# Dividing a finished attention block: from a ScalarE copy, a VectorE reciprocal and a GpSimd product to VectorE alone, straight from PSUM

## The reference

```python
scores = jnp.einsum('bhnd,bhmd->bhnm', q, k) / sqrt(Dh)
attn = jax.nn.softmax(scores, axis=-1)
sa = jnp.einsum('bhnm,bhmd->bhnd', attn, v)
sa = sa.transpose(0, 2, 1, 3).reshape(bs, N, H * Dh)
out = jnp.einsum('bnd,ed->bne', sa, w_agg) + b_agg
```

## Time and profile before

| what | value |
|---|---|
| median of 3 runs | 1554.31 us (1553.98 to 1554.68) |
| the profiled execution's own time | 1566.26 us |
| its span, first to last instruction | 1564.0 us |
| mean granted TensorE clock | 0.934 of full speed |
| busy: PE, DVE, ACT, POOL | 1364.3, 1062.3, 869.9, 564.2 us |
| instructions: PE, DVE, ACT, POOL | 10311, 2037, 1251, 1142 |

### The profile page before, as it was taken

How to read it: one execution, slowest core, us unless ns; L and a number is a source line. 1 busy time by engine, 2 the same in 40 slices (tenths; PEclk the granted TensorE clock), 3 DMA queues, 4 the chain that set the end, 5 groups by cost and what they waited for, 6 DMA issues and landing times.

```text
span 1564.0 us, 27948 instructions
## 1 busy us (share of the span) xinstructions
PE 1364.3 (87%) x10311; PEld 912.5 (58%) x10311; DVE 1062.3 (68%) x2037; ACT 869.9 (56%) x1251; POOL 564.2 (36%) x1142
## 2 busy tenths in 40 slices
PE   4777989999999999999999999999988988886563
PEld 3534555666566666665666566656655555564452
DVE  3325684859585958596858685868598899746711
ACT  1244656666767666766666666666646555521110
POOL 1311530335133503350345034503431051656663
PEclk8888999999999999999999999999999988978775
DMA  2034002600360036013500360036000640344442
GB/s 74 2 92 110 1 28 64 181 14 15 80 178 14 28 71 173 14 29 80 164 14 28 80 164 14 28 78 166 14 1 16 160 135 1 109 149 137 127 138 69
DMA packets 66014, 119.07 MB, mean 76 GB/s; under 512 B 10321, under 2 KB 46162, under 8 KB 65874
## 3 DMA queue, kind: packets, MB, share of 16 engines
q1 hardware_dynamic: 56640, 92.04, 22.1%
q0 software_dynamic: 8192, 25.17, 5.3%
q10 hardware_dynamic: 1042, 0.01, 0.0%
HBM read 29.11 MB, written 33.55 MB: 40 GB/s over the span
## 4 chain that ended last, share of the span: by engine, by line
PE 55%; DVE 22%; issue 7%; ACT 5%; POOL 4%; SPq 2%; another core or an unknown queue 2%; DMA 1%; DVEq 0%; ACTq 0%; POOLq 0%
PE shared L873 29%; PE scores L829 10%; PE acc L851 9%; DVE prob_sum L1489 9%; PE shared L868 3%; ACT probs L1123 3%; DVE acc_sb L1474 2%; PE acc L861 2%; PE acc L848 1%; DVE bn L1249 1%; DVE best_i L1406 1%; DVE work L1408 1%; DVE best L1404 1%; SPq L465 1%
## 5 line engine op out<-in xcount | busy, mean ns | idle before, releaser
L1123 ACT ACTIVATE probs<-scores 128x1024 f32<-128x1024 f32 x512 | 516.0, 1022 | 218.6 <-DVE prob_sum L1489 127.7
L1489 DVE TENSOR_TENSOR prob_sum<-prob_sum,probs 128x512 f32<-128x512 f32 x640 | 420.6, 717 | 0.3 <-issue 0.3
L829 PE MATMUL scores<-query_stack,key_stack 96*128 96x256 f32 x2048 | 344.6, 308 | 49.5 <-ACT probs L1123 45.5
L829 PEld LDWEIGHTS scores<-query_stack,key_stack 96*128 96x128 f32 x2048 | 278.7, 194 | 125.6 <-ACT probs L1123 77.4
L851 PE MATMUL acc<-probs,v_all 128*32 128x256 f32 x4096 | 296.2, 397 | 0.0
L1156 POOL TENSOR_TENSOR attn_T<-acc_sb 128x256 f32<-128x256 f32 x64 | 55.5, 866 | 522.7 <-DVE acc_sb L1474 515.5
L873 PE MATMUL shared<-w_sb,chan 128*128 128x512 f32 (+1 forms) x512 | 185.4, 503 | 5.3 <-DVE chan L1310 5.0
L851 PEld LDWEIGHTS acc<-probs,v_all 128*32 128x32 f32 x4096 | 116.0, 112 | 98.2 <-issue 31.2
L1489 DVE TENSOR_TENSOR prob_sum<-probs 128x512 f32<-128x512 f32 x128 | 97.0, 799 | 59.3 <-PE acc L861 55.3
L873 PEld LDWEIGHTS shared<-w_sb,chan 128*128 128x128 f32 x512 | 92.8, 193 | 66.3 <-issue 56.5
L1474 DVE RECIPROCAL acc_sb<-acc_sb 128x256 f32<-128x256 f32 x64 | 111.5, 1742 | 26.6 <-ACT acc_sb L1113 26.5
(11 more groups left out here) (168 smaller groups left out, 1955.9 us busy)
## 6 DMA issues: line engine op xcount, KB each, us to landing
query_stack<-hi SPq DMA_DIRECT2D x128, 128.0 KB, 2.4
key_stack<-hi SPq DMA_DIRECT2D x128, 128.0 KB, 2.5
x_sb<-in_x_dram SPq DMA_DIRECT2D x8, 1024.0 KB, 5.8
key_stack<-lo SPq DMA_DIRECT2D x64, 128.0 KB, 2.5
query_stack<-lo SPq DMA_DIRECT2D x64, 128.0 KB, 2.5
out_dram<-resid SPq DMA_DIRECT2D x16, 512.0 KB, 4.9
tokens_scratch<-resid SPq DMA_DIRECT2D x16, 512.0 KB, 6.3
tokens_scratch<-rows SPq DMA_DIRECT2D x16, 512.0 KB, 6.5
```

Of the source, the lines that this page charges most:

```text
L829: last = pe.matmul(score_ps[u % 2][:, QB * r:QB * (r + 1)], key_stack[stack, HG * g + r, P * kt:P * (kt + 1)], query_stack[stack, HG * g + ...
L1123: act.activation(probs[:, u % PROBS, :], score_ps[u % 2][:, :], ACT.Exp, scale=DH ** -0.5) \
L1489: dve.tensor_tensor(total[:, part], probs[:, (u - 1) % PROBS, part] if kt == 1 else total[:, part], probs[:, u % PROBS, part], ALU.add).th ...
```

## The change

VectorE's `divide` takes the place of three pieces: `copy_acc` on ACT, `invert` on DVE and `divide` on POOL. It waits for `blocks_done`, takes the reciprocal of the bank's right half from PSUM into a new small buffer `sum_r`, waits for its own `recip_ready`, and multiplies the bank's left half, again from PSUM, with `sum_r` into `attn_T`. PE waits for `attn_ready` where it waited for `acc_copied`. For the first four blocks of a batch it must not overwrite `attn_T` while `agg` of the batch before reads it: POOL waited, at the first of them, for the last two tiles of `agg`; DVE waits at each of the four for the two tiles that this block overwrites.

```diff
@@ tensor: weigh
                 if kt == 0 and blk >= 2:
-                    pe.wait_ge(s["acc_copied"], blk - 1)
+                    pe.wait_ge(s["attn_ready"], blk - 1)
@@ scalar
-            def copy_acc(blk):
-                act.wait_ge(s["blocks_done"], blk + 1)
-                await_count(act, "attn_ready", blk)
-                act.activation(acc_sb[:, :], acc_ps[blk % 2][:, :], ACT.Copy) \
-                   .then_inc(s["acc_copied"], 1)
...
-                if k and k % BLOCK_PAIRS == 0:
-                    copy_acc(k // BLOCK_PAIRS - 1)
@@ gpsimd
-            def divide(blk):
-                a, g, qb = blk // (G * NQB), blk % (G * NQB) // NQB, blk % NQB
-                pool.wait_ge(s["recip_ready"], blk + 1)
-                if a and blk % (G * NQB) == 0:
-                    storing = next(seg for seg in segments if seg.has("store") and seg.stores == a - 1)
-                    for t in range(T - 2, T):
-                        await_read(pool, storing, "agg", t)
-                pool.tensor_tensor(attn_T[:, g, QB * qb:QB * (qb + 1)], acc_sb[:, 0:QB],
-                                   acc_sb[:, QB:2 * QB], ALU.mult).then_inc(s["attn_ready"], 1)
...
-                if k and k > BLOCK_PAIRS and k % BLOCK_PAIRS == 1:
-                    divide(k // BLOCK_PAIRS - 1)
@@ vector
-            def invert(blk):
-
-                dve.wait_ge(s["acc_copied"], blk + 1)
-                dve.reciprocal(acc_sb[:, QB:2 * QB], acc_sb[:, QB:2 * QB]).then_inc(s["recip_ready"], 1)
+            def divide(blk):
+                a, g, qb = blk // (G * NQB), blk % (G * NQB) // NQB, blk % NQB
+                dve.wait_ge(s["blocks_done"], blk + 1)
+                if a and g == 0:
+                    storing = next(seg for seg in segments if seg.has("store") and seg.stores == a - 1)
+                    for t in range(QB // P * qb, QB // P * (qb + 1)):
+                        await_read(dve, storing, "agg", t)
+                acc = acc_ps[blk % 2]
+                dve.reciprocal(sum_r[:, :], acc[:, QB:2 * QB]).then_inc(s["recip_ready"], 1)
+                dve.wait_ge(s["recip_ready"], blk + 1)
+                dve.tensor_tensor(attn_T[:, g, QB * qb:QB * (qb + 1)], acc[:, 0:QB], sum_r[:, :], ALU.mult) \
+                   .then_inc(s["attn_ready"], 1)
...
                 if k and k % BLOCK_PAIRS == 0:
-                    invert(k // BLOCK_PAIRS - 1)
+                    divide(k // BLOCK_PAIRS - 1)
```

More of the change, by code:

```diff
@@ L360, in build_attention @@
     prob_sum = sb("prob_sum", [P, HG * QB])
-    acc_sb = sb("acc_sb", [P, BANK])
+    sum_r = sb("sum_r", [P, QB])
     head_ones = env["head_ones"]
@@ L417, in build_attention @@
              "stats_ready x_stats_ready z2_ready maxima_ready resid_ready dve_done one_row_in summed "
-             "blocks_done acc_copied norm_squared bound_ready shift_known attn_ready recip_ready").split()
+             "blocks_done norm_squared bound_ready shift_known attn_ready recip_ready").split()
     sems = {n: ctx.enter_context(nc.semaphore(n)) for n in names}
@@ L660, in build_segments @@
      qT, z2T, qk0, dots_sb, sumv_sb, x_sum, bn6, bn_x, mv, mv_x, small, ss, hr, hh, ln_v, ln_r, ln_h, ln_b,
-     prob_sum, acc_sb, head_ones, norm_sq, norm_max, pair_max, bound, shifted, logits_sb, score_ps, acc_ps,
+     prob_sum, sum_r, head_ones, norm_sq, norm_max, pair_max, bound, shifted, logits_sb, score_ps, acc_ps,
      shared_ps) = (env[k] for k in (
@@ L664, in build_segments @@
         "qT z2T qk0 dots_sb sumv_sb x_sum bn6 bn_x mv mv_x small ss hr hh ln_v ln_r ln_h ln_b "
-        "prob_sum acc_sb head_ones norm_sq norm_max pair_max bound shifted logits_sb score_ps acc_ps "
+        "prob_sum sum_r head_ones norm_sq norm_max pair_max bound shifted logits_sb score_ps acc_ps "
         "shared_ps").split())
@@ L1133, in _ @@
                     exponential(2 * k + 2)
-                elif units and n and plan[n - 1].pair == pairs - 1:
-                    copy_acc(units // T - 1)
                 for st in first:
@@ L1234, in _ @@
                 k = slot.pair
-                if units and k is None and n and plan[n - 1].pair == pairs - 1:
-                    divide(units // T - 1)
-                if k and k > BLOCK_PAIRS and k % BLOCK_PAIRS == 1:
-                    divide(k // BLOCK_PAIRS - 1)
                 for st in slot.steps:
@@ L1495, in _ @@
                 if units and k is None and n and plan[n - 1].pair == pairs - 1:
-                    invert(units // T - 1)
+                    divide(units // T - 1)
                 for st in first:
```

## The result

The changed kernel took 1561.6 us (median of 11 runs, 1558.0 to 1563.2), the kernel before 1554.3 us (median of 11, 1550.5 to 1559.3): a ratio of 1.0043, 95% interval 1.0031 to 1.0056. On another chip, where the kernel before stood at 1575.0 us, the ratio was 1.0052 (1.0035 to 1.0070). The change makes the kernel some 7 us slower.

A forecast was written before the change was run, and what follows sets the result against it. PE was taken as the bound in the long run, with the chain often leaving it for DVE; +10.4 (DVE's product) - 2.4 (copy wait) - 1.7 (POOL relief) = +6.3 us on 1554.3 gave 1560.6 us, range 1553 to 1567.

The forecast's parts named there:

- DVE's product: The division's multiply, moved to DVE: +0.45 us for each block, +10.4 us over 23 places on the chain.
- The 23 places: Blocks of 64 whose reciprocal stands on the chain, two in each repeating segment (slots 0 and 12); each pays 0.45 us.
- the rival of the absorbed delay: Chain places in repeating segments run into cover the chain doesn't show: sum +1.8 us, 1556.1 us, no change; chance 0.26.
- the ten places: Chain places in the repeating segments after the first segment; without them the sum was put at 6.3 - 4.5 = +1.8 us.
- The pause that it named: PE's idle time at the end of slot 12's chain, 0.78 us before, expected near 1.2 after.
- POOL's product: 64 x 866 ns leave POOL, 55.5 us; claimed that nothing on the chain gets earlier by that alone.
- The relief term of -1.7 us: DVE's sums no longer stretched 0.46 us beside POOL's product, at four chain places in the last three segments and the first.
- PSUM: Reading reciprocal and product operands from PSUM: taken as 0, bounds -0.7 to +2.6 us over the 23 places.
- The rival of dear PSUM reads: Reciprocal and product each cost 57 ns more from PSUM: +2.6 us, 1563.2 us, or 1567.3 without relief; chance 0.12.
- The wait for the copy: DVE no longer waits for ACT's copy; gains at three chain places (192.88, 1356.68, 1367.39 us), -2.4 us in sum.
- Its rival: DVE's 26.5 us of waiting for the copy reaches PE; with half of it 1549.7 us, faster; chance 0.12.
- PE's new wait for `attn_ready`: PE waits for the block two back, set three slots ahead; costs nothing unless DVE falls back by three slots.

The follow-up runs named there:

- The doubled product: Changed kernel, with each block's product made a second time by DVE into a tile that nothing reads; ratio 1.0153 to the kernel before, body 1013.5 us.

## Why the prediction was right, and where its steps failed

The time (1560.6 forecast, 1561.6 measured) and the sign came out. That the number is so near is luck: the stretch that the profile can compare has +8.0 us in the repeating segments, where the forecast has +5.4, and -1.7 in the rest up to the last `total`, where it has +0.9. The two misses cancel.

- **DVE's product, +0.45 us at a place on the chain.** Right as a price: 0.42 us from a row of 0.41, and at slot 0 it gave +0.51 us in each segment, with PE's wait at 1.02 us for a forecast of 0.95. The doubled product gave 0.29 to 0.34 us more in the periods where the clock stayed up.
- **The count of places on the chain.** The 23 places are those of one chain, and the prediction put the 41 others beside other work. The doubled product reached PE in slots 4, 20 and 24 of the repeating segments too, and in the changed profile the chain goes over the division in slot 24 of five of these segments and in slot 12 of none. So a chain names one of several paths of nearly the same length. In the rival of the absorbed delay the ten places are twelve by the prediction's own count of two in each of six segments, which makes its sum +0.9 us and not +1.8.
- **Slot 12: wrong in size.** The same step said +0.45 us each; measured +0.8 in two segments and +2.2 in four. The step added a duration to a chain and took all other durations as given. The pause that it named stayed at 0.78 us (it expected 1.2); the one before it grew by 0.56, from 0.16 to 0.72. Of the +0.8, then, 0.56 is that pause and 0.23 or more POOL. The rest of the +2.2 is the granted clock, 1.37 us for each fall to 0.50, and those falls need the grown pause: with it filled there was none.
- **Slots 20 to 24: not in the sum.** -4.4 us over five segments, since the clock no longer fell there. Why it falls in one place or the other is not settled. The runs show that it was never both: in 14 profiles with five segments each, no segment has a fall in slots 12 to 16 and in slots 20 to 24. The pauses of slots 20 to 24 are 0.77, 0.65 and 1.01 us in the changed kernel, without a fall, and the same with slot 13's pause filled or moved, with a fall in three of the five segments. Over the repeating segments the two terms nearly bring the sum back to the forecast's (+8.0 for +5.4), and no step of the forecast had earned that.
- **POOL's product.** The prediction said that its removal brings nothing on the chain forward by itself. It brought POOL's head scaling forward by 1.8 us onto DVE's sums. The relief term of -1.7 us has the right size by coincidence: it was meant for four places in the first and the last three segments, and what the ruler shows lies elsewhere. Slots 4 to 8 gained 1.5 us in six segments, and with the product back they grew by 0.09 of the 0.20 us a time, so about half of that gain is the contention, and what else it is stays open. The Trainium skill's rule of "SBUF — State Buffer", section "Who interferes with whom", that a VectorE instruction with two SBUF inputs and a GpSimd one that reads SBUF shut each other out, agrees with the ten sums of 8.51 us beside the head scaling and 6.82 with that held back.
- **PSUM.** 0 was right: +3 ns on the reciprocal, -6 on the product. The rival of dear PSUM reads falls. The 62 cycles, 65 ns, that the Trainium skill's page "VectorE: DVE Perf Modes" gives in its section on the TRN2 errata do not show in these instructions.
- **The wait for the copy, -2.4 us.** With the copy kept the body was 1.7 us longer and the rest up to the last block 2.0 us. That lies near the forecast, but runs with the same code differed by 4 us in the body, so the size isn't shown. Its rival falls: of the 25.6 us of waiting that came back, half would have shown as 13 us.
- **PE's new wait for `attn_ready`** cost nothing, as said, and 17.7 us once the division came three slots later, which is the bound that the prediction named.

## What to carry to other kernels

Price a moved instruction by where it stands as well as by its length: here 0.56 us more of waiting, next to another pause under 1 us, led to 1.37 us of lost clock, so look at the granted clock by windows behind each pause that an edit lengthens. Work taken from an engine off the chain lets its next step start earlier; ask beside what. A chain is one path: places that it leaves out can be nearly as tight. And before work is moved "to where there is slack", follow what each engine has queued behind it, and what will run beside it: a division of 2.1 us came back as a pause of 6.2.

## What the runs showed of the hardware

Four transposes more, 0.43 us of TensorE's work in a pause, made each of six periods 1.37 us shorter. The granted clock fell to 0.50 for 3.4 us behind pauses of 0.72 and 0.78 us, in four of six places in one profile and six of six in another of the same kernel (0.16 and 0.78 did not do it in this place), and pauses of 1.03 and 0.78 us were followed by a fall in only two of six segments. The Trainium skill's page "TensorE: Matmul & The Clock Gate", section "A second HAM failure mode: psum-queue depth-cycling", tells of a kernel whose short idle times between groups of matmuls make the clock swing between its two levels; these traces agree, with falls in slots 12 to 16, where no pause is longer than 0.79 us. Matmuls of the same form took 0.61 us for a group of eight at 1.00 and 1.10 at 0.50.
